# Inverse norms of the local layers' queries and keys: VectorE's reciprocal and ScalarE's square root in place of GpSimd's power

## What is computed

```python
def l2norm(t):
    return t / jnp.maximum(jnp.linalg.norm(t, axis=-1, keepdims=True), 1e-12)

def attn_layer(x, Wqkv, qs, ksc, Wo):          # 16 heads of 64
    q, k, v = jnp.split(x @ Wqkv, 3, -1)       # then split into heads
    q, k = l2norm(q) * qs, l2norm(k) * ksc
    q = q * cos * scale + rotate_half(q) * sin * scale
    k = k * cos * inv + rotate_half(k) * sin * inv
    return local_attention(q, k, v) @ Wo       # windows of 32, softmax(8 q k)

for i in range(6):
    x = attn_layer(shift_tokens(x), Wqkv[i], q_scale[i], k_scale[i], Wo[i]) + x
    x = ffn_layer(shift_tokens(x), ln_g[i], ln_b[i], W1[i], b1[i], W2[i], b2[i]) + x
```

## Time and profile before

| | before |
|---|---|
| median of 3 runs | 4593.13 us (4592.19 to 4593.53) |
| span of the profiled execution | 4596.8 us |
| PE busy in the span | 4085.1 us (89%) |
| DVE | 3862.2 us (84%) |
| POOL | 3640.7 us (79%) |
| ACT | 3501.9 us (76%) |
| the pow of line 1585 | 192 instructions, 1138.8 us |

### The profile page before, as it was taken

How to read it: one execution, slowest core, us unless ns; L and a number is a source line. 1 busy time by engine, 2 the same in 40 slices (tenths; PEclk the granted TensorE clock), 3 DMA queues, 4 the chain that set the end, 5 groups by cost and what they waited for, 6 DMA issues and landing times.

```text
span 4596.8 us, 140828 instructions
## 1 busy us (share of the span) xinstructions
PE 4085.1 (89%) x57664; PEld 3035.9 (66%) x57664; DVE 3862.2 (84%) x6471; ACT 3501.9 (76%) x6378; POOL 3640.7 (79%) x2624
## 2 busy tenths in 40 slices
PE   7987466557885999999999999999999999999997
PEld 5665345445663667776777767776777777777776
DVE  4664999864555989998999989998999989999994
ACT  4664788874543778887888888887888878888885
POOL 1111888863337999998999999998999999999994
PEclk9999788888997999999999999999999999999999
DMA  2000000000000222222222222222222222222222
GB/s 64 2 2 1 1 1 1 1 1 28 2 2 8 53 55 54 64 66 57 56 60 73 54 61 54 64 69 55 57 59 73 54 61 54 64 70 59 55 58 62
DMA packets 120845, 198.83 MB, mean 43 GB/s; under 512 B 66896, under 2 KB 78224, under 8 KB 120080
## 3 DMA queue, kind: packets, MB, share of 16 engines
q1 hardware_dynamic: 120208, 189.82, 16.7%
HBM read 24.12 MB, written 2.10 MB: 6 GB/s over the span
## 4 chain that ended last, share of the span: by engine, by line
PE 61%; DVE 13%; POOL 12%; issue 8%; ACT 5%; DMA 0%; DVEq 0%; POOLq 0%; SPq 0%; ACTq 0%
PE ps L1306 7%; PE ps L1250 7%; PE ps L1251 6%; PE ps L1317 6%; PE ps L1278 4%; PE ps L1297 3%; PE ps L1290 3%; PE ps L1358 3%; PE ps L1298 3%; POOL arena L1585 3%; POOL arena L1590 2%; PE ps L1347 2%; PE ps L1341 2%; PE ps L1259 2%; DVE arena L1512 2%
## 5 line engine op out<-in xcount | busy, mean ns | idle before, releaser
L1585 POOL TENSOR_TENSOR arena<-arena 128x32 f32<-128x32 f32 x192 | 1138.8, 5931 | 72.3 <-DVE arena L1498 72.3
L1590 POOL TENSOR_TENSOR arena<-arena 128x1024 f32<-128x1024 f32 x384 | 907.1, 2362 | 11.0 <-DVE arena L1489 10.9
L208 POOL TENSOR_SCALAR arena<-arena 128x2 f32<-128x2 f32 x256 | 72.5, 283 | 645.6 <-DVE arena L202 634.4
L1376 ACT ACTIVATE arena<-ps 128x1024 f32<-128x1024 f32 x384 | 391.1, 1021 | 198.3 <-PE ps L1251 193.3
L1488 DVE TENSOR_TENSOR arena<-ps,arena 128x1024 f32<-128x1024 f32 x384 | 468.5, 1220 | 79.6 <-ACT arena L1376 73.3
L1608 POOL TENSOR_TENSOR arena<-arena 128x1536 f32<-128x1536 f32 x192 | 529.0, 2755 | 1.8 <-DVE arena L1522 1.8
L1489 DVE TENSOR_TENSOR arena<-ps,arena 128x1024 f32<-128x1024 f32 x384 | 466.5, 1215 | 0.0
L1306 PEld LDWEIGHTS ps<-arena 96*64 96x64 f32 x12288 | 385.4, 138 | 115.5 <-issue 115.3
L1496 DVE TENSOR_REDUCE arena<-arena 128x32 f32<-128x2048 f32 x192 | 437.0, 2276 | 0.0
L1250 PE MATMUL ps<-arena 128*128 128x512 f32 x768 | 414.5, 622 | 18.4 <-DVE arena L1514 15.8
L1397 ACT ACTIVATE arena<-arena 128x96 f32<-128x96 f32 x1536 | 427.1, 368 | 2.4 <-DVE arena L1514 2.4
(11 more groups left out here) (252 smaller groups left out, 9793.2 us busy)
## 6 DMA issues: line engine op xcount, KB each, us to landing
arena<-arena SPq DMA_DIRECT2D x192, 384.0 KB, 4.3
arena<-arena SPq DMA_DIRECT2D x192, 256.0 KB, 3.7
arena<-arena SPq DMA_DIRECT2D x192, 128.0 KB, 2.3
arena<-in_dWqkv SPq DMA_DIRECT2D x18, 512.0 KB, 3.6
arena<-arena SPq DMA_DIRECT2D x96, 64.0 KB
arena<-arena SPq DMA_DIRECT2D x96, 63.5 KB
arena<-in_dWo SPq DMA_DIRECT2D x6, 512.0 KB, 5.8
arena<-in_x SPq DMA_DIRECT2D x4, 512.0 KB, 7.4
```

The lines of the kernel that those rows point to most:

```text
L1585: pool.tensor_tensor(ss[:, 0:32], ss[:, 32:64], mhalf32, ALU.pow).then_inc(*S.rs.up())
L1590: pool.tensor_tensor(a1[:, half], a1[:, half], T2[:, half], ALU.add).then_inc(*radd[g].up())
```

## The change

The pow of POOL and the constant mhalf32 go. On DVE, ssum gets a third instruction, a reciprocal of 128x32 in place, which waits for the maximum ahead of it. On ACT a new piece, rt, takes the square root of it into ss[:, 0:32]. Since 1/x and then the root is x to the power of minus one half, the factors are the same but for rounding. All who waited for rs (nrm0 on POOL, nrm1 and ssum on DVE, ex0 on ACT) wait for rt. rs stood at 1496 in the table, rt stands at 1620, which on ACT is between the sq0 and the sq1 of the next tile. Lines of the changed kernel are up to 7 higher or lower than those of before.

```diff
-            "rs": 1496, "radd1": 1632, ...
+            "rt": 1620, "radd1": 1632, ...
...
         def tile(piece, l, k):          # act_program
...
+            if piece == "rt":
+                if n >= 3:
+                    act.wait_ge(*S.nrm_q.at(n - 2))
+                    act.wait_ge(*S.nrm_k.at(n - 2))
+                act.wait_ge(*S.ssum.at(n + 1))
+                act.activation(SS[n % 3][:, 0:32], SS[n % 3][:, 32:64], ACT.Sqrt).then_inc(*S.rt.up())
...
             if piece == "ssum":         # dve_program
...
-                dve.tensor_scalar(ss[:, 32:64], ss[:, 32:64], 1e-24, None, ALU.max).then_inc(*S.ssum.up())
+                dve.tensor_scalar(ss[:, 32:64], ss[:, 32:64], 1e-24, None, ALU.max).then_inc(*S.step_dve.up())
+                dve.wait_ge(*S.step_dve.now())
+                dve.reciprocal(ss[:, 32:64], ss[:, 32:64]).then_inc(*S.ssum.up())
...
-            if piece == "rs":           # pool_program
-                if n >= 3:
-                    pool.wait_ge(*S.nrm_q.at(n - 2))
-                    pool.wait_ge(*S.nrm_k.at(n - 2))
-                    pool.wait_ge(*S.ex0.at(n - 2))
-                pool.wait_ge(*S.ssum.at(n + 1))
-                pool.tensor_tensor(ss[:, 0:32], ss[:, 32:64], mhalf32, ALU.pow).then_inc(*S.rs.up())
```

More of the change, by code:

```diff
@@ L694, in pool_program @@
         if first:
-            pool.memset(K.mhalf32, -0.5)
             pool.memset(mhalf, -0.5).then_inc(*S.step_pool.up())
@@ L1173, in phase_d @@
     pe, act, dve, pool, sp = C.pe, C.act, C.dve, C.pool, C.sp
-    XR, XX, ident, identb, maskd, mhalf, mhalf32 = K.XR, K.XX, K.ident, K.identb, K.maskd, K.mhalf, K.mhalf32
+    XR, XX, ident, identb, maskd, mhalf = K.XR, K.XX, K.ident, K.identb, K.maskd, K.mhalf
     L, wqkv, wo, w1, w2, b1, ln, rope, scb = W.L, W.wqkv, W.wo, W.w1, W.w2, W.b1, W.ln, W.rope, W.scb
@@ L1179, in phase_d @@
         "step_dve step_pool sh_ps q_ps k_ps qt_ps kt_ps s0_ps s1_ps p0_ps p1_ps v_ps o_ps wo_ps ft_ps fg_ps fa_ps fo_ps",
-        "xs sq_q sq_k qT kT ex0 ex1 pT0 pT1 vn oT fn fzT fge en",
+        "xs sq_q sq_k rt qT kT ex0 ex1 pT0 pT1 vn oT fn fzT fge en",
         "ro_q ro_k ssum nrm_q nrm_k sub0 sub1 rc xxa fone fstat fgm xxf estat xe",
-        "rs radd_q radd_k halo pn frs tab ers zeroed",
+        "radd_q radd_k halo pn frs tab ers zeroed",
         "v0 v1 fs0 fs1 fs2 stored")
@@ L1393, in tile @@
                 if g == 0:
-                    act.wait_ge(*S.rs.at(n + 1))
+                    act.wait_ge(*S.rt.at(n + 1))
                     for x in range(8):
@@ L1494, in tile @@
                 if n >= 3:
-                    dve.wait_ge(*S.rs.at(n - 2))
+                    dve.wait_ge(*S.rt.at(n - 2))
                 dve.tensor_reduce(ss[:, 32:64], SQ.rearrange("p (h e) -> p h e", h=32), AX.X, ALU.add).then_inc(*S.step_dve.up())
                 dve.wait_ge(*S.step_dve.now())
-                dve.tensor_scalar(ss[:, 32:64], ss[:, 32:64], 1e-24, None, ALU.max).then_inc(*S.ssum.up())
+                dve.tensor_scalar(ss[:, 32:64], ss[:, 32:64], 1e-24, None, ALU.max).then_inc(*S.step_dve.up())
+                dve.wait_ge(*S.step_dve.now())
+                dve.reciprocal(ss[:, 32:64], ss[:, 32:64]).then_inc(*S.ssum.up())
             if piece == "nrm1":
-                dve.wait_ge(*S.rs.at(n + 1))
+                dve.wait_ge(*S.rt.at(n + 1))
                 dve.wait_ge(*S.radd_k.at(n + 1))
@@ L1591, in tile @@
             if piece == "nrm0":
-                pool.wait_ge(*S.rs.at(n + 1))
+                pool.wait_ge(*S.rt.at(n + 1))
                 pool.wait_ge(*S.radd_q.at(n + 1))
@@ L1809, in network @@
         identb, mask, maskd = sb([128, 128], BF16), sb([128, 2, 128], BF16), sb([128, 2, 384], BF16)
-        mhalf, mhalf32 = sb([128, 2]), sb([128, 32])
+        mhalf = sb([128, 2])
         base = C.top
@@ L1815, in network @@
         ld_id, ld_m, ld_d, masks = C.loads("ld_id ld_m ld_dm masks")
-        Shared = namedtuple("Shared", "XR XX ident identb mask maskd mhalf mhalf32 base ld_x ld_id ld_m ld_d masks stage_m stage_d")
-        K = Shared(XR, XX, ident, identb, mask, maskd, mhalf, mhalf32, base, ld_x, ld_id, ld_m, ld_d, masks, stage_m, stage_d)
+        Shared = namedtuple("Shared", "XR XX ident identb mask maskd mhalf base ld_x ld_id ld_m ld_d masks stage_m stage_d")
+        K = Shared(XR, XX, ident, identb, mask, maskd, mhalf, base, ld_x, ld_id, ld_m, ld_d, masks, stage_m, stage_d)
         la, lb, lc = load_a(C, K), load_b(C, K), load_c(C, K)
```

## The result

| | before | changed |
|---|---|---|
| median | 4593.33 us (4592.19 to 4596.11, 4 runs) | 5085.51 us (5084.67 to 5086.65, 4 runs) |
| ratio | 1 | 1.107, 95% interval 1.1054 to 1.1086 |
| span of the profiled execution | 4596.8 us | 5083.4 us |

The change costs 492 us, or 10.7%. The prediction had 65 us and a range that ended at 4740. What it named as the cost, ScalarE's table loads, is not what costs here.

What follows compares the result with a forecast made beforehand. TensorE was taken as the bound. 64 us from ScalarE's loads, 3 from stalls and 2 from VectorE, minus 4 at GpSimd's start, gave plus 65 us: median from 4593 to 4658 us, range 4605 to 4740.

Steps and rivals of the forecast that it cites:

- The bound: Local layers: TensorE bounds the kernel, busy 98% of 2920 us; other engines could give back only 59 us there.
- idle time of TensorE that VectorE ends: Sign of being wrong: TensorE idle before pieces other than s1 of tile A and fo, released by VectorE.
- GpSimd: the pow goes: Repeating entry: 192 pows of 5.9 us leave an engine TensorE doesn't wait for, worth 0; 4 us off once at start.
- The rivals: Alternatives for the time: closed ScalarE queue 0.20, slack holds the loads 0.10, doubled load 0.03, faster without layer stalls 0.04.
- A load costs twice what its row shows: Rival on ScalarE: Sqrt's load needs the engine emptied or a longer copy; plus 320 us, 4910; chance 0.03.
- ScalarE: the loads: ScalarE: 293 more table loads, 4.6 us of work an entry with the roots; TensorE loses 0.7 us an entry, 64 us.
- the copies of p0 and p1: Sign of being right: they release TensorE's new idle time before s1 of tile A and before fo.
- The walk through ScalarE's list: One entry followed through ScalarE's queue: TensorE 0.45 us late in tile A, another 0.15 to 0.3 at fo in B.
- VectorE: a reciprocal comes: VectorE: 0.29 us more a tile, hidden where ScalarE or TensorE is last; 2 us in the phase's first tiles.
- TensorE's clock: Local layers: granted clock 0.99 of full speed, so TensorE's busy time is its work and not its clock.
- The start of the phase: First nrm0, for which TensorE waited 13.86 us: without the pow before it, 4 us off, once.
- The stalls at a layer's tables: Five TensorE stalls of about 7.2 us stay, as GpSimd awaits scb's load; each grows about 0.6 us, 3 us.

Runs made afterwards that it cites:

- the multiplication of 128x2304: Run with the pow put back into a spare buffer, but for five layers a GpSimd multiplication reading and writing SBUF replaces that pow: 4831.45 us.
- the last run: The kernel before, with GpSimd making the next layer's tables at 17500 instead of 16000 and their load issued as before: 4552.97 us, ratio 0.9904.

## Why the prediction was wrong, point by point

**The bound: right for the kernel before.** TensorE was the bound, and no run with GpSimd freed of the pow came in below it. In the changed kernel VectorE holds TensorE up. The prediction had named that as a sign of being wrong: idle time of TensorE that VectorE ends.

**"GpSimd: the pow goes ... worth 0": this step failed.** It asked who waits for GpSimd and not what GpSimd does to VectorE while both run. Taking the pow away didn't only free time. It moved radd1 and pn, which read SBUF from end to end, from behind the pow to right behind ro1, where VectorE has its maximum and nrm1. 390 us of the 492 came off when the pow was put back. TensorE's busy time fell by 185 us with it, so about half of the price comes by way of its slow clock behind the waits. The trace before had a sign of it, which I didn't read. One line's durations (min/median/max in ns), the maximum before the change:

```profile
L1498 DVE TENSOR_SCALAR arena<-arena x192: 180/212/1672, 1418.9 to 4484.6; 128x32 f32<-128x32 f32 x192
```

This instruction of fixed size takes 180 ns at best and 1672 at worst: in each of the 26 cases of 0.25 us or more it ended 0.03 to 0.05 us after a radd or an nrm0 of GpSimd that ran beside it. It was waiting inside its own duration. The Trainium skill has the rule, in "SBUF — State Buffer", section "Who interferes with whom": a VectorE instruction with two SBUF inputs contends with a GpSimd one that reads SBUF, tensor_scalar on SBUF can take the shared ports too, and whoever issues first blocks the other for the whole instruction. The rows above agree for radd1, pn and the multiplication of 128x2304. They differ for the pow, which waited for nrm1 when it came second, and didn't block it for the whole instruction when it came first. That was what made the old order work.

**The rivals: none of them was it.** "A load costs twice what its row shows" gave the time nearest to the measured one, 4910, by a mechanism that wasn't there: the mean of 149 loads of the root is 1283 ns.

**"ScalarE: the loads", 0.7 us an entry: size near in one setting, place wrong.** With the pow in place the loads cost 78 us, 0.8 us an entry, and part of that was the maximum's block. Without the maximum and with pn early they cost 13. Nor did TensorE wait for the copies of p0 and p1. In the kernel with pow and loads its waits, 2000 to 4500 us, were:

```profile
PE ps L1272 <- DVE arena L1534: 31.5, 74, 0.6
PE ps L1290 <- DVE arena L1546: 30.1, 64, 0.6
```

xxa and fgm of VectorE. The load ahead of the second squaring delays it, then ro1, ssum and what stands behind. The walk through ScalarE's list looked at the slots that ScalarE frees and left VectorE's out. And in the changed kernel itself the loads cost 5 us, within the scatter, since VectorE was later still. That the 78 us were near the forecast is luck in part.

**"VectorE: a reciprocal comes", 2 us: mis-sized.** It takes 353 ns for 128x32, where 253 for 128x16 had been taken over without regard to size, and together with ScalarE's short instruction it came to 25 us and not 2. "Hidden" was wrong, because xxa stands right behind it: in the run with pow and without loads TensorE waited 19.0 us for xxa, in 77 places (2000 to 4500 us).

**TensorE's clock: left out.** The prediction took it as fixed at 0.99. Behind two waits of 1.4 us close together it was at 0.51, and the entry shown lost about as much to that (5.95 us in all, less 3.0 of waits) as to the waits themselves.

**The start of the phase: right.** TensorE's first wait for nrm0 is 10.03 us in the changed kernel, where it was 13.86, and 4 us had been taken off.

**The stalls at a layer's tables: right that they stay**, 36.5 us in five places where it was 35.8, and the last run shows the DMA to be the reason. They didn't grow by 0.6 us each.

## What to carry to other kernels

Before an instruction is taken off GpSimd, look at what will then stand in its time and what VectorE does beside it: a long GpSimd instruction can be a shield if VectorE runs undisturbed beside it, as beside this pow. Read the spread of a line's durations and not the mean alone: here the long tail of a fixed-size instruction was a block. And where such a block is found, moving one piece in the list can be worth more than a saved instruction: pn a tile earlier gave 292 us and cost nothing.

## What the runs showed of the hardware

- A GpSimd tensor_tensor on SBUF and a VectorE tensor_tensor with both inputs in SBUF, or a tensor_scalar on SBUF, exclude each other by whole instructions: nrm1 1.22 us alone, 3.31 behind pn; the 128x2304 multiplication 4.03 us alone, 5.08 behind nrm1.
- GpSimd's pow of 128x32 doesn't hold nrm1 up when it began first (5.45 us, nrm1 1.22 beside it), and is held up by nrm1 when it began second (6.46 us).
- A tensor_scalar over 33 elements is blocked as one over 32 is (1080 and 1081 ns).
- A reciprocal on VectorE took 253 ns for 16 elements a partition and 353 for 32, beside pn too (352 to 356 ns over all 192).
- The root of 128x32 takes 0.23 us on ScalarE, its table load 1283 ns, whatever was loaded before.
- TensorE's granted clock was 0.50 over 3026 to 3028 us and 0.51 over 3028 to 3032, behind a wait of 1.48 us that followed one of 1.37 by 1.7 us, and 1.00 over 3032 to 3033, after 6 us of unbroken work. In the run with pn early a wait of 1.38 us for xxa stands alone in the entry, and the clock was 0.99 over 2000 to 4500 us.
